# The expert layer of a two-block decoder: four experts a turn, against pairs of experts with packed gate and up products

## What is computed

```python
logits = x @ gate_w.T; probs = softmax(logits); scores, idx = top_k(probs, 8)   # 64 experts
xbuf = zeros((64, C, 256)).at[e_sorted, pos].set(x[tok_sorted], mode='drop')
g = einsum('ecd,efd->ecf', xbuf, w_gate)      # f = 96
u = einsum('ecd,efd->ecf', xbuf, w_up)
y = einsum('ecf,edf->ecd', silu(g) * u, w_down)
out = zeros((N, 256)).at[tok_sorted].add(y[e_sorted, pos] * scores)
```

## Time and profile before

| what | value |
|---|---|
| median of 3 runs | 4114.34 us |
| profiled execution, own time | 4120.83 us |
| its span | 4119.1 us |
| busy over the span: PE, DVE, ACT, POOL | 83%, 60%, 45%, 48% |
| expert part: first DMA issue to last scatter | 3509.6 to 4003.9 us |
| sum part | 4012.1 to 4119.1 us |

### The profile page before, as it was taken

How to read it: one execution, slowest core, us unless ns; L and a number is a source line. 1 busy time by engine, 2 the same in 40 slices (tenths; PEclk the granted TensorE clock), 3 DMA queues, 4 the chain that set the end, 5 groups by cost and what they waited for, 6 DMA issues and landing times. The chain is left out here.

```text
span 4119.1 us, 101732 instructions
## 1 busy us (share of the span) xinstructions
PE 3422.2 (83%) x37378; PEld 2298.8 (56%) x37378; DVE 2477.5 (60%) x4566; ACT 1839.7 (45%) x4960; POOL 1975.5 (48%) x2832
## 2 busy tenths in 40 slices
PE   8996899673799999999999999999927886788860
PEld 6774666442566666666666666666614443455530
DVE  4563565131677777777777777777736774233326
ACT  1111455111566666666666666666614443222220
POOL 2332332230565665665656655656533655355541
PEclk9998899785999999999999999999957776899985
DMA  2001552101111111111111111111026541555534
GB/s 73 15 10 36 129 125 56 53 10 54 48 46 47 52 37 50 48 44 53 45 37 55 45 43 54 44 45 47 27 65 139 137 126 67 151 154 154 156 97 173
DMA packets 268892, 293.40 MB, mean 71 GB/s; under 512 B 93988, under 2 KB 237032, under 8 KB 261768
## 3 DMA queue, kind: packets, MB, share of 16 engines
q1 hardware_dynamic: 250024, 252.40, 22.3%
q0 software_dynamic: 18432, 34.96, 2.4%
HBM read 170.71 MB, written 132.12 MB: 74 GB/s over the span
## 5 line engine op out<-in xcount | busy, mean ns | idle before, releaser
L1793 PE MATMUL head_ring<-gd_xT,head_w 128*128 128x512 f32 x1024 | 518.5, 630 | 22.6 <-POOL head_eye L2226 19.9
L1282 POOL DMA_INDIRECT ytok<-exp_y,exp_cur x256 | 249.0, 973 | 253.8 <-ACT exp_y L1240 182.5
L2201 POOL TENSOR_TENSOR head_V<-head_V,gd_ones 128x512 bf16<-128x512 f32 x128 | 133.0, 1040 | 473.9 <-DVE head_V L2074 473.9
L2049 DVE SCALAR_TENSOR_TENSOR head_cb_V<-head_ring,head_taps,head_cb_V 128x504 f32<-128x504 f32 (+2 forms) x384 | 279.9, 729 | 12.2 <-ACT head_cb_V L1938 7.5
L1793 PEld LDWEIGHTS head_ring<-gd_xT,head_w 128*128 128x128 f32 x1024 | 179.2, 195 | 159.2 <-issue 129.0
L1912 PE MATMUL head_by<-head_wo,head_ogT 128*128 128x256 f32 x1024 | 258.0, 395 | 9.5 <-issue 6.0
L1802 PE MATMUL head_ring<-head_w,gd_xT 128*128 128x256 f32 x1024 | 256.6, 394 | 2.2 <-DVE head_cb_V L2049 2.2
L2080 DVE TENSOR_TENSOR head_Xs<-head_bx,head_join 128x512 bf16<-128x512 f32 x320 | 220.0, 687 | 60.1 <-PE head_bx L1834 54.1
L1912 PEld LDWEIGHTS head_by<-head_wo,head_ogT 128*128 128x128 f32 x1024 | 186.7, 192 | 40.1 <-issue 14.6
L1975 ACT CAST head_Tt<-head_btt 128x512 bf16<-128x512 f32 x320 | 191.1, 597 | 35.6 <-PE head_btt L1842 34.1
L1802 PEld LDWEIGHTS head_ring<-head_w,gd_xT 128*128 128x128 f32 x1024 | 184.8, 190 | 34.4 <-DVE head_cb_V L2049 2.6
(11 more groups left out here) (350 smaller groups left out, 9249.1 us busy)
## 6 DMA issues: line engine op xcount, KB each, us to landing
xbuf<-head_blank SPq DMA_DIRECT2D x64, 552.0 KB
exp_xg<-xbuf SPq DMA_DIRECT2D x64, 552.0 KB
head_gi<-scan SPq DMA_DIRECT2D x64, 256.0 KB
ytok<-head_blank SPq DMA_DIRECT2D x64, 256.0 KB
sum_yg<-ytok SPq DMA_DIRECT2D x16, 1024.0 KB, 5.1
cb_Q<-qd SPq DMA_DIRECT2D x48, 192.0 KB
cb_K<-kd SPq DMA_DIRECT2D x48, 192.0 KB
cf_Q<-qd SPq DMA_DIRECT2D x48, 192.0 KB
```

What stands on the lines that cost most here:

```text
L1282: pool.indirect_dma_start(ytok, bass.IndirectOffsetOnAxis(ap=cur[e][:, b:b + 1], axis=0), y[e][:, b, :], None, bounds_check=ROWS * K - 1, ...
L1793: last = pe.matmul(b[:, :], w[:, c, FEAT[what]], xT[:, c, n % UNITS * N:n % UNITS * N + N], start=c == 0, stop=c == DC - 1)
L2049: dve.scalar_tensor_tensor(out=out, in0=by_seq(bank_of(f, n))[:, :, 0:SEQ - s], scalar=taps[:, TAP[f], KS - 1 - s:KS - s], in1=out, op0=AL ...
```

## The change

The experts go in 32 pairs, s = 0, 1 in a pair, and all loops are unrolled in Python.

- Layout of the weights: `moe_w` holds for a pair three blocks of 128 columns. Block 0 is the 96 columns of gate of expert 0 and the last 32 of its up; block 1 is the last 32 of gate, the last 32 of up and the first 64 of gate of expert 1; block 2 is the first 64 of up of expert 0 beside the first 64 of up of expert 1. `moe_wd` has 128 rows an expert, in the order in which `h` has them; 32 rows are zero, and `h` is zero there from a memset at the start.
- PE, per pair: `pgu[s]` = block s, all 128 columns (L1226); `pu`, one bank for both, rows 0 to 63 from expert 0 and rows 64 to 127 from expert 1, each matmul with 64 columns (L1230), the two experts in turn; then the 16 transposes of the next pair (L1212); then down of both experts, with 128 rows of `h` (L1243).
- ACT: silu is two instructions for an expert (L1264, 64 and 32 rows), with a shift of partitions for 32 of them. ACT also takes one of the two copies to `xgT[s]` (L1253); DVE keeps the other (L1283).
- DVE: `h` is two instructions for an expert, 32 rows from `pgu` (L1301) and 64 rows from `pu` (L1304). The shares come once in two pairs, and only they wait for `rank_in`.
- Down of expert s of pair i also waits until both copies of pair i+1 are made, since its banks are those of the transposes.
- SP: per pair two loads of slots, one of `moe_w` (393 KB, 3072 bytes a partition, L1172) and two of `moe_wd` (131 KB each, L1177), two pairs ahead, each behind the event that frees its buffer.
- POOL's scatters are the same 4 for an expert (L1327). `cur` has 4 sets of buffers, `y` as before 4 experts.

```diff
-            GROUP = 4
-            TURNS = E // GROUP
-            G = range(GROUP)
...
+            PAIRS = E // 2
+            B = S = range(2)
+            AHEAD = 4
...
+            UP = (slice(0, SEQ), slice(SEQ, P))
+            GATE = (((slice(0, 64), slice(0, 64)), (slice(64, 96), slice(96, 128))), ((slice(64, 128), slice(64, 128)), (slice(0, 32), slice(32, 64))))
+            LATE = (slice(96, 128), slice(32, 64))
+            EMPTY = (slice(64, 96), slice(0, 32))
...
+                    for i in range(PAIRS - 2):
+                        for s in S:
+                            sp.wait_ge(cur_ready[s], START + i + 1)
+                            sp.wait_ge(x_filled[s], START + i + 1)
+                            inputs(i + 2, s)
+                        sp.wait_ge(u_filled, START + i + 1)
+                        upper(i + 2)
+                        for s in S:
+                            sp.wait_ge(y_filled[s], START + i + 1)
+                        lower(i + 2)
...
+                    def turn_over(i):
+                        for s in S:
+                            pe.wait_ge(x_in[i % 2][s], START + i // 2 * 16 + 16)
+                            if i >= 2:
+                                pe.wait_ge(y_ready[s], START + i - 1)
+                            for c in range(DC):
+                                for b in range(QB):
+                                    last = pe.transpose(pxy[s][c][:, b * P:b * P + P], xg[i % 2][s][:, b, c * P:c * P + P], ident[:, :])
+                            last.then_inc(x_filled[s], 1)
+
...
+                    for i in range(PAIRS):
+                        pe.wait_ge(w_in[i % 2], START + i // 2 * 16 + 16)
+                        for s in S:
+                            pe.wait_ge(x0_ready[s], START + i + 1)
+                            pe.wait_ge(x1_ready[s], START + i + 1)
+                            if i:
+                                pe.wait_ge(h_ready[s], START + i)
+                                pe.wait_ge(late_ready[s], START + i)
+                            for c in range(DC):
+                                last = pe.matmul(pgu[s][:, :], w[i % 2][:, c, s, :], xgT[s][:, c, :], start=c == 0, stop=c == DC - 1)
+                            last.then_inc(g_filled[s], 1)
+                        for c in range(DC):
+                            for s in S:
+                                last = pe.matmul(pu[UP[s], :], w[i % 2][:, c, 2, UP[s]], xgT[s][:, c, :], start=c == 0, stop=c == DC - 1,
+                                                 skip_group_check=True)
+                        last.then_inc(u_filled, 1)
+                        if i + 1 < PAIRS:
+                            turn_over(i + 1)
+                        pe.wait_ge(wd_in[i % 2], START + i // 2 * 32 + 32)
+                        for s in S:
+                            pe.wait_ge(h_ready[s], START + i + 1)
+                            pe.wait_ge(late_ready[s], START + i + 1)
+                            if i + 1 < PAIRS:
+                                pe.wait_ge(x0_ready[s], START + i + 2)
+                                pe.wait_ge(x1_ready[s], START + i + 2)
+                            for b in range(QB):
+                                last = pe.matmul(pxy[s][b // 2][:, b % 2 * D:b % 2 * D + D], h[s][:, b * P:b * P + P], wd[i % 2][s][:, :],
+                                                 start=True, stop=True)
+                            last.then_inc(y_filled[s], 1)
...
+                    def half(i, s):
+                        act.wait_ge(x_filled[s], START + i + 1)
+                        if i:
+                            act.wait_ge(u_filled, START + i)
+                        act.copy(xgT[s][:, 1, :], pxy[s][1][:, :]).then_inc(x1_ready[s], 1)
+
+                    for s in S:
+                        half(0, s)
+                    for i in range(PAIRS):
+                        for s in S:
+                            act.wait_ge(g_filled[s], START + i + 1)
+                            if i:
+                                act.wait_ge(h_ready[s], START + i)
+                                act.wait_ge(late_ready[s], START + i)
+                            for source, target in GATE[s]:
+                                last = act.activation(act_g[s][target, :], pgu[s][source, :], ACT.Silu)
+                            last.then_inc(g_ready[s], 1)
+                        if i + 1 < PAIRS:
+                            for s in S:
+                                half(i + 1, s)
+                        for s in S:
+                            act.wait_ge(y_filled[s], START + i + 1)
+                            if i >= 2:
+                                act.wait_ge(y_free[s], START + i - 1)
+                            for c in range(DC):
+                                last = act.copy(y[i % 2][s][:, 2 * c:2 * c + 2, :].rearrange("p b d -> p (b d)"), pxy[s][c][:, :])
+                            last.then_inc(y_ready[s], 1)
...
+                    def half(i, s):
+                        dve.wait_ge(x_filled[s], START + i + 1)
+                        if i:
+                            dve.wait_ge(u_filled, START + i)
+                        dve.tensor_copy(xgT[s][:, 0, :], pxy[s][0][:, :]).then_inc(x0_ready[s], 1)
+                        if i >= AHEAD:
+                            dve.wait_ge(y_free[s], START + i - AHEAD + 1)
...
+                    for i in range(PAIRS):
+                        for s in S:
+                            dve.wait_ge(g_ready[s], START + i + 1)
+                            if i:
+                                dve.wait_ge(y_filled[s], START + i)
+                            else:
+                                dve.wait_ge(blank, START + 2)
+                            dve.tensor_tensor(h[s][LATE[s], :], pgu[s][LATE[s], :], act_g[s][LATE[s], :], ALU.mult).then_inc(late_ready[s], 1)
+                        for s in S:
+                            dve.wait_ge(u_filled, START + i + 1)
+                            dve.tensor_tensor(h[s][UP[s], :], pu[UP[s], :], act_g[s][UP[s], :], ALU.mult).then_inc(h_ready[s], 1)
+                            if i + 1 < PAIRS:
+                                half(i + 1, s)
...
+    moe_w = np.stack([np.concatenate([wg[0::2], wu[0::2, 64:96]], axis=1),
+                      np.concatenate([wg[1::2, 64:96], wu[1::2, 64:96], wg[1::2, 0:64]], axis=1),
+                      np.concatenate([wu[0::2, 0:64], wu[1::2, 0:64]], axis=1)], axis=1)
+    moe_w = moe_w.reshape(32, 3, P, DC, P).transpose(0, 4, 3, 1, 2)
+    moe_wd = np.zeros((64, P, D), wd.dtype)
+    moe_wd[0::2, 0:64], moe_wd[0::2, 96:128] = wd[0::2, 0:64], wd[0::2, 64:96]
+    moe_wd[1::2, 64:128], moe_wd[1::2, 32:64] = wd[1::2, 0:64], wd[1::2, 64:96]
```

More of the change, by code:

```diff
@@ L1119, in stage_moe @@
 def stage_moe(nc, src, dst, ctxt, qd, kd, xbuf, ytok, A):
[L1121 removed]
+    E, K, CAP = Rows.E, Rows.K, Rows.CAP
     QB = CAP // P
@@ L1152, in stage_moe @@
-            w_in, x_in, sent, free = m.sems("w_in", GROUP), m.sems("x_in", GROUP), m.sems("sent", GROUP, 0), m.sem("free")
-            y_free = m.sems("y_free", GROUP)
-            x_filled, g_filled, u_filled, y_filled = (m.sems(n, GROUP) for n in ("x_filled", "g_filled", "u_filled", "y_filled"))
-            g_ready, y_ready = m.sems("g_ready", GROUP), m.sems("y_ready", GROUP)
-            x_ready, h_ready, cur_ready = m.sems("x_ready", GROUP), m.sems("h_ready", GROUP), m.sems("cur_ready", GROUP)
+            pgu, pu = [m.ps(f"pgu{s}") for s in S], m.ps("pu")
@@ L1176, in _ @@
                     inputs(0, 1)
-                    weights(0, 0)
-                    weights(0, 1)
-                    for e in (2, 3):
-                        inputs(0, e)
-                        weights(0, e)
-                    sp.dma_start(rank[:, :], A["rank"]).then_inc(rank_in, 16)
-                    with sp.Fori(0, TURNS - 1) as turn:
-                        for what, e in events:
-                            if what == "X":
-                                sp.wait_ge(cur_ready[e], START + turn + 1)
-                                sp.sem_inc(free, 1)
-                                inputs(turn + 1, e)
-                            elif what == "Y":
-                                sp.wait_ge(y_filled[e], START + turn + 1)
-                                sp.sem_inc(free, 1)
-                                weights(turn + 1, e)
@@ L1193, in _ @@
-                    for e in G:
-                        sp.wait_ge(sent[e], TURNS * QB * 16)
+                    upper(0)
+                    lower(0)
+                    for s in S:
+                        inputs(1, s)
+                    upper(1)
+                    lower(1)
+                    sp.dma_start(rank[:, :], A["rank"]).then_inc(rank_in, 16)
+                    for i in range(PAIRS - 2):
[8 more added lines that the diff above has]
+                        lower(i + 2)
@@ L1226, in _ @@
                 @block.scalar
                 def _(act):
```

(16 more changed lines are left out.)

151 lines of the change are left out of this document (62 added, 89 removed).

## The result

The changed kernel takes 4077.3 us (median of 10 runs, 4069.1 to 4087.5), the kernel before 4109.0 beside it (10 runs, 4096.6 to 4122.8): a ratio of 0.992, 95% interval 0.9907 to 0.9932. That is 32 us less, where 131 were predicted; 4077 lies above the range of 3960 to 4040.

A forecast was written before the change was run, and what follows sets the result against it. TensorE was taken to bound the expert part. Start 3519.2 + 2.5, 31 pairs of 10.7, then 9.2 + 10.2 end at 3872.8, 131 us less than 4003.9: 3985 us in all (-3.1%), range 3960 to 4040 (8 in 10).

The forecast's parts named there:

- TensorE's work: TensorE's products and transposes for a pair of experts were to sum to 10.63 us against 12.20, 50 us less in all.
- runs in twos: On TensorE, the side-by-side product's half-width records overlap, 1.90 us; rival: one after the other, 3.63 us, total 4040, chance 0.07.
- The schedule of a pair: Almost all TensorE waiting in a pair goes, about 0.1 us stays: 10.7 us; a pair of 10.4 to 11.2 had 0.77.
- with 0.05 us from an end to the start that waits for it: In a pair's schedule, each engine was to start 0.05 us after the end it waits for, read ahead of one product.
- not due before 8.98: Down product of a pair's second expert: its copies were wanted by 8.6 us, before TensorE would reach it at 8.98.
- a chain of 12 us: Rival: a chain through VectorE, ScalarE or GpSimd ends later, a pair takes 12 us, total 4027 us, chance 0.08.
- Start: At the expert part's start, TensorE was to begin 5.7 us earlier, with 2.5 us put for the lower clock.
- DMA: Expert part's loads and writes: 73 MB at 212 GB/s, share 0.70, no waits counted; rival DMA bound, 4055 us, chance 0.03.
- The clock: Rival: TensorE stays at 1.2 GHz in much of the expert part, a pair costs 10.6 us more; 18 give 4180; chance 0.03.
- The 131 us: Total gain claimed for the expert part: its end at 3872.8 us against 4003.9 before.

The follow-up runs named there:

- e11: The changed kernel, unaltered, on a chip where the kernel before takes 4071.7 us: 3971.7 us, ratio 0.9748.
- e9: The changed kernel, unaltered, as a control on a chip where the kernel before takes 4105.4 us: 4068.9 us, ratio 0.9903.
- e16: The changed kernel with a GpSimd wait that holds back the second expert's four scatters: 4071.0 us against 4134.2 for the kernel before, ratio 0.9841.
- e2: The kernel before without its 256 indirect DMAs of the expert part: 4058.8 us, against 4074.2 for the kernel before unaltered.
- e8: The kernel before with weights loaded for the first turn only: 4063.9 us, against 4074.7 for the kernel before unaltered.
- e10: The kernel before, unaltered, run again for its trace: 4098.7 us, with 4105.4 for the kernel before beside it.
- e15: The changed kernel without the expert part's indirect DMAs: 3991.5 us, on a chip where the kernel before takes 4134.2 us.
- e3: The changed kernel with each expert's four indirect DMAs replaced by two plain DMAs from GpSimd's queue: 3965.6 us, against 4074.2 for the kernel before.
- e5: The changed kernel with the gate and up weight load issued later, behind the waits for both down products: 3973.4 us, ratio 0.9747 to the kernel before.
- e13: The changed kernel with the gate and up weight load issued later, behind the down products: 3972.2 us, ratio 0.9741 to the kernel before.
- e14: The changed kernel with a GpSimd wait that cuts the burst of eight scatters into two of four: 3970.5 us, ratio 0.9744 to the kernel before.

## Why the prediction failed, point by point

- **TensorE's work: right, by a size.** The side-by-side product runs in twos: 3526.67 - 3524.80 = 1.87 us for 8 records (1.90 predicted). The Trainium skill's rule that loads overlap only where the row group differs ("TensorE: Matmul & The Clock Gate", What overlaps and what doesn't) does not hold for these halves; the measurement decides. Gate product and down 3.53 each (3.47 and 3.46). From the first of the 16 transposes to the down product 3520.38 - 3518.30 = 2.08 us go by, not 1.80. The transposes themselves are as fast as before; the down product waits for VectorE's copy of expert 0:

```profile
3519.43 0.69 DVE L1283 COPY exp_xgT<-exp_pxy 128x512 f32<-128x512 f32 x1 [0.27 <-PE exp_pxy L1212]
```

 It ends at 3520.12, 7.2 behind the pair's first product (7.15 predicted), but the down product starts 0.26 later, and not 0.05. In e11, e9, e16 and the first result this distance is 0.26 in every pair, also where the copy itself is late. So the 0.05 of rows 5 was too little here as well; what makes up the 0.26 no run separates. Sum 11.00 instead of 10.63.
- **The schedule of a pair: right where signals are prompt.** On chips P and Q, and on S without scatters, TensorE works through 11.00 us with no other wait than the one just named. GpSimd, at 10.2 of 11.0, did no harm there.
- **The step that failed: "with 0.05 us from an end to the start that waits for it".** It came from one place, ahead of the first scatter. On the chip that took the first result, signals of TensorE in the last third of a burst of eight scatters are answered up to 3.9 us late, 3.6 in the pair shown. The down product of the second expert, "not due before 8.98", then starts 11.94 after the pair's first product (3533.22 - 3521.28), and the part is 460.7 - 370.5 = 90 us longer than in e11. I had a chain of 12 us at 0.08, with "engines react late in the loops of before" for it, and dismissed it by looking at GpSimd's issue time alone.
- **The trace of before had it.** I read only TensorE's rows of the turn. Beside them stand:

```profile
3675.96 1.88 PE L1217 MATMUL exp_pg<-exp_xgT,exp_wg 128*96 128x512 f32 x4
...
3678.91 0.59 ACT L1235 ACTIVATE exp_act_g<-exp_pg 96x512 f32<-96x512 f32 x1 [1.62 <-PE exp_pg L1217]
...
3679.39 1.89 PE L1222 MATMUL exp_pxy<-exp_wd,exp_h 96*128 96x256 f32 x8
...
3681.82 1.07 ACT L1240 COPY exp_y<-exp_pxy 128x512 f32<-128x512 f32 x2 [2.32 <-PE exp_pxy L1222]
```

 The product ends at 3677.84 and its silu starts 1.07 later on an idle ScalarE; the down product ends at 3681.28 and is copied 0.54 later. In e2, without scatters, the same copy starts 0.04 behind:

```profile
3673.93 1.89 PE L1222 MATMUL exp_pxy<-exp_wd,exp_h 96*128 96x256 f32 x8
...
3675.86 1.07 ACT L1240 COPY exp_y<-exp_pxy 128x512 f32<-128x512 f32 x2 [2.85 <-PE exp_pxy L1222]
...
3677.08 1.06 PE L1209 MATMUL exp_pxy<-moe_ident,exp_xg 128*128 128x128 f32 x8 [1.25 <-ACT exp_y L1240]
```

 and the 1.76 us in the bracket of rows 3 is 1.25. The kernel before paid 0.5 us there. In the changed kernel the signal is 3.6 us late and the pair 2.7 us longer (13.7 against 11.00), since its second copy waits for a signal that falls into the end of a burst of eight, and since TensorE does its work in order and all that follows stands behind that wait. In the kernel before, the last scatter of that burst (at 3679.22, 0.97 long) had ended 1.1 us ahead of the down product, so a signal can be late just behind a burst as well.
- **Start: right, and 2 us better.** The first product comes 3489.77 - 3482.32 = 7.5 us behind the first load in e11 and 7.9 in the first result (9.6 predicted, 15.4 before).
- **DMA: right to leave out.** In e11 the part has a share of 0.61 and 200 GB/s (0.70 and 212 predicted), and no wait for a load but the first.
- **The clock: right.** 0.98 over the part in e11, with its 16 transposes in a row, 0.94 in the first result, whose TensorE idles a fifth of the time. The Trainium skill's rule that transposes do not count as activity as other matmuls do ("TensorE: Matmul & The Clock Gate", PE-mode transpose) changed nothing that could be read here.
- **The 131 us.** On the quick kind the part takes 3482.32 to 3852.77, 370.5 us; I had 363.2. The 7 more are 30 pairs of 0.30 (11.00 for 10.7), and small ends of both signs. The gain there is still only 100 us, since the kernel before is itself quicker on such a chip: 370.5 + 100 makes its part 470 us, by subtraction, against the 494.3 of the late chip. e8, the kernel before without most weight loads, has its part at 471.6 on Q. So of the 131, 100 are there where signals are prompt, 24 were the late chip's share in the kernel before, 7 were my sum. Of the 24, 16 turns of 0.5 are late signals by themselves; TensorE's busy time in e8 is 403.55 us against 417.08 in rows 1, with a granted clock of 0.97 against 0.95, and whether that loss of clock follows from the late waits is not shown. The other trace of before on a late chip, e10, has a part of 489.2 us, so some 5 of the 24 may be no more than the spread of single executions.

Windows of e11 and of e15 (no scatters, late chip), columns as above:

```profile
3482.00:3853.00 371.00, 351.35 (x1536) 216.16 (x1536) 172.69 (x306) 183.03 (x321) 252.15 (x256) 0.98 0.61 200
```
```profile
3515.00:3880.00 365.00, 352.18 (x1536) 216.19 (x1536) 172.64 (x306) 182.91 (x321) 0.00 (x0) 0.98 0.48 158
```

**What stays open.** Why chips differ, and what in making or carrying out indirect DMAs holds the signal of TensorE, while those of ScalarE come in 0.03 us. Whether e3's plain writes from GpSimd would be late on chips R and S is not known, since e3 ran on P, where nothing is late. No version here is shown to beat the changed kernel: e5, e13 and e14 equal it on the quick kind, and e16's 0.984 on S stands beside 0.990 and 0.992 of the unaltered kernel on other chips, which is no comparison.

## What to carry to other kernels

Before you schedule to tenths of a microsecond, compare in the trace each end of a producer with the start of its idle reader, in the busiest stretch and not in the first: a reader that starts late behind a finished producer is a price that grows when the stretch gets denser. Where a wait is labelled with a transfer that ended long ago, ask what signal was late. And put the unaltered kernel beside every edit on the same chip; two batches of mine "confirmed" a cause that was only another chip.

## What the chip did that I had not expected

Signals of TensorE were late only in or just behind a stretch with indirect DMAs from GpSimd, and only on some chips. A difference between the kinds shows in an earlier part too: up to the first of the 128 scatters into `xbuf`, in the router part, the changed kernel is equally far on both kinds; that row and the last of them, on the late chip of e9 and then in e11:

```profile
3180.95 1.20 POOL L893 DMA_INDIRECT xbuf<-moe_row,cf_to  x1 [0.41 <-issue]
...
3497.61 0.98 POOL L893 DMA_INDIRECT xbuf<-moe_row,cf_to  x1 [0.30 <-issue]
```
```profile
3179.05 1.20 POOL L893 DMA_INDIRECT xbuf<-moe_row,cf_to  x1 [0.41 <-issue]
...
3474.33 0.97 POOL L893 DMA_INDIRECT xbuf<-moe_row,cf_to  x1 [0.30 <-issue]
```

After three milliseconds the two are 1.9 us apart, then they take 316.7 against 295.3 us for the same scatters. In all traces this is 310 to 324 us on the late kind (six) and 287 to 297 on the quick kind (fourteen); that late signals are the cause there too was not looked into. The longest delay of the first result stands where the scatters of two pairs run together, fifteen in one run:

```profile
3722.23 3.60 PE L1226 MATMUL exp_pgu<-exp_xgT,exp_w 128*128 128x512 f32 x8
...
3733.40 0.97 POOL L1327 DMA_INDIRECT ytok<-exp_y,exp_cur  x1 [0.30 <-issue]
...
3735.50 1.19 ACT L1264 ACTIVATE exp_act_g<-exp_pgu 64x512 f32<-64x512 f32 x2 [3.77 <-DMA cf_c<-ctxt]
```

The product ends at 3725.83 and the silu of the second expert starts 9.7 us later, 1.1 us behind the last of the fifteen; the next pair begins at 3744.61, after 22.4 us. Where sixteen run together, in the last two pairs, it is 8.8. And the pause: a fill of 0.56 us keeps GpSimd from its next scatter for 1.5 us instead of 0.3.
